# A windowed attention block with MLP: who issues the shift rows and bias rows, and in what order the last stage's data are loaded

## The reference, cut to what matters

```python
B, H, W, C = 8, 16, 16, 192; HEADS = 12; KD = 16; WS = 14; MLP_DIM = 768
h = layer_norm(x, ln1_g, ln1_b)
hp = pad(h, to 28 x 28)                       # 4 windows of 14 x 14 for each image
q, k, v = windows(hp) @ qkv_w + qkv_b         # 12 heads of 16 channels
attn = (q * KD ** -0.5) @ k.T + bias_h[..., :, None] + bias_w[..., None, :]
                                              # bias_h, bias_w: q times relative tables
o = softmax(attn) @ v
x2 = x + unwindow(o @ proj_w + proj_b)
out = x2 + gelu(layer_norm(x2, ln2_g, ln2_b) @ mlp_w1 + mlp_b1) @ mlp_w2 + mlp_b2
```

## Time and profile before

| | us |
|---|---|
| median of 3 runs | 299.33 |
| lowest, highest | 298.60, 302.65 |
| the profiled execution's own time | 298.07 |
| its span in the profile | 296.3 |

### The profile page before, as it was taken

How to read it: one execution, slowest core, us unless ns; L and a number is a source line. 1 busy time by engine, 2 the same in 40 slices (tenths; PEclk the granted TensorE clock), 3 DMA queues, 4 the chain that set the end, 5 groups by cost and what they waited for, 6 DMA issues and landing times.

```text
span 296.3 us, 5322 instructions
## 1 busy us (share of the span) xinstructions
PE 259.4 (88%) x1980; PEld 201.0 (68%) x1980; DVE 164.6 (56%) x435; ACT 128.5 (43%) x233; POOL 92.7 (31%) x143
## 2 busy tenths in 40 slices
PE   0499979899969999999998995899788599999995
PEld 0445458897656777777775673468467478889995
DVE  4875476335686888887887782255499312011011
ACT  1244674433545776676665574352001653141300
POOL 7258480103000333324564412950057700000000
PEclk9999997999977999999998999569557999999999
DMA  6544003374712776777646648601000000101011
GB/s 183 158 120 115 5 2 81 75 173 117 164 39 67 167 175 164 189 183 189 165 134 165 154 82 244 184 19 31 0 0 1 0 2 0 53 2 53 0 55 53
DMA packets 22303, 27.90 MB, mean 94 GB/s; under 512 B 7147, under 2 KB 18515, under 8 KB 22277
## 3 DMA queue, kind: packets, MB, share of 16 engines
q1 hardware_dynamic: 19477, 24.90, 33.3%
q0 software_dynamic: 2272, 2.46, 3.5%
q10 hardware_dynamic: 528, 0.20, 0.3%
HBM read 5.81 MB, written 1.57 MB: 25 GB/s over the span
## 4 chain that ended last, share of the span: by engine, by line
PE 63%; DVE 11%; SPq 10%; DMA 6%; ACT 4%; issue 3%; ACTq 2%; DVEq 0%
PE ps L1289 11%; PE ps L1274 9%; PE ps L977 7%; PE ps L1012 6%; PE ps L1131 5%; PE ps L1067 4%; PE ps L1107 4%; DMA rd<-kst 3%; PE ps L1032 3%; SPq L345 2%; ACT pm L612 2%; DMA qop<-bias 2%; PE ps L1178 2%; DVE var L906 2%; SPq L382 2%
## 5 line engine op out<-in xcount | busy, mean ns | idle before, releaser
L799 DVE TENSOR_REDUCE nmax<-ps 98x2 f32<-98x392 f32 x96 | 52.9, 565 | 24.3 <-PE ps L1067 22.6
L612 ACT ACTIVATE pm<-ps 98x784 f32<-98x784 f32 x48 | 38.9, 825 | 22.7 <-PE ps L1107 22.7
L1067 PE MATMUL ps<-kop,qop 126*98 126x196 f32 x192 | 37.7, 282 | 3.4 <-DMA qop<-bias 1.7
L1067 PEld LDWEIGHTS ps<-kop,qop 126*98 126x98 f32 x192 | 26.3, 171 | 10.3 <-DVE nmax L799 4.1
L1289 PE MATMUL ps<-w2t,gl 128*128 128x192 f32 x192 | 31.7, 326 | 0.0
L1289 PEld LDWEIGHTS ps<-w2t,gl 128*128 128x128 f32 x192 | 31.4, 190 | 0.3
L1107 PE MATMUL ps<-qop,kop 128*98 128x196 f32 x192 | 28.2, 272 | 3.0 <-DMA qop<-shift 2.3
L675 ACT ACTIVATE gl<-ps,b 128x512 f32<-128x512 f32 x24 | 16.4, 688 | 26.5 <-PE ps L1274 26.1
L477 POOL DMA_DIRECT2D den<-osb x11 | 7.1, 643 | 63.1 <-ACT osb L625 63.1
L1107 PEld LDWEIGHTS ps<-qop,kop 128*98 128x98 f32 x192 | 23.1, 180 | 5.0 <-DMA qop<-shift 2.6
L1131 PE MATMUL ps<-pm,v_main 128*17 128x196 f32 x384 | 23.3, 365 | 3.1 <-ACT pm L612 3.0
(11 more groups left out here) (132 smaller groups left out, 458.8 us busy)
## 6 DMA issues: line engine op xcount, KB each, us to landing
qop<-bias SPq DMA_DIRECT2D x8, 343.0 KB
qop<-hl SPq DMA_DIRECT2D x12, 196.0 KB
kop<-hl SPq DMA_DIRECT2D x12, 196.0 KB
bias<-in_x SPq DMA_DIRECT2D x4, 384.0 KB, 4.6
xres<-in_x SPq DMA_DIRECT2D x2, 768.0 KB, 7.9
out<-xn SPq DMA_DIRECT2D x8, 192.0 KB, 2.0
kop<-kst SPq DMA_DIRECT2D x3, 477.8 KB
ot<-osb POOLq DMA_DIRECT2D x44, 32.0 KB, 2.2
```

Source lines behind the costliest of these rows:

```text
L612: a.activation(pm[0:HALF, gi], ps[0:HALF, b0:b0 + 2, 0:2 * WIN], ACT.Exp).then_inc(s["exp_done"], 1)
L799: v_.tensor_reduce(nmax[0:HALF, h % 2, 2 * n:2 * n + 2], ps[0:HALF, bank, 0:2 * WIN].rearrange("p (t k) -> p t k", t=2), AX.X, ALU.max, ne ...
L1067: o = mm(ps[0:HALF, bank, WIN * t:WIN * (t + 1)], q[0:R_MAX, WIN * n + HALF * t:WIN * n + HALF * (t + 1)], kk[0:R_MAX, WIN * n:WIN * (n + ...
```

## The change

Four things are done.
- ScalarE no longer issues the shift rows' transfers; GpSimd does both (`place_main_shifts`, `place_rest_shifts`). Its order in step h is: output of head h − 1, main shift of head h + 1, main low biases of head h + 3, rest shift of head h + 1, rest biases of head h + 3.
- For heads 8 to 11 the high bias rows of the rest half are issued by GpSimd too, which makes four transfers there; SyncE's rest half has four transfers instead of six.
- SyncE loads selector, bias vectors and first projection weight, then the denominators' rows, then w1 and the second projection weight, then the residual in two halves and w2, each of the last three with a semaphore of its own. Who needs the residual waits for it half by half, TensorE waits for w2 at the second layer.
- VectorE takes the last reciprocals at u = 1 instead of u = 5.

```diff
@@ -162,7 +162,7 @@
-            "st_done", "exp_done", "pv_done", "osb_ready", "o_in", "o_in1", "late_in", "rden_ready", "bc_done",
+            "st_done", "exp_done", "pv_done", "osb_ready", "o_in", "o_in1", "late_in", "x_late0_in", "x_late1_in", "w2_in", "rden_ready", "bc_done",
@@ -181,6 +181,7 @@
+        x_late_in = [s["x_late0_in"], s["x_late1_in"]]
@@ -267,15 +268,15 @@
                 (dst[r0:r0 + KD, QUAD * j:QUAD * (j + 1)], osb[32 * j:32 * j + KD, h % 2]) for j in range(4)]
-        def low_biases_loaded(h):
-
-            return 32 * len(range(h, A8 - 1, -RING))
-
-        def operands_loaded(h):
-
-            return 16 * sum(5 if n < A8 else 6 for n in range(h % RING, h + 1, RING))
-
-        N_LATE, N_HIDDEN = 6 * 16, 5 * 16
+        def low_biases_loaded(h, part):
+
+            return 32 * (part + 1) * len(range(h, A8 - 1, -RING))
+
+        def operands_loaded(h, part):
+
+            return 16 * sum(5 if n < A8 else (6, 4)[part] for n in range(h % RING, h + 1, RING))
+
+        N_LATE, N_HIDDEN = 4 * 16, 4 * 16
         block = ctx.enter_context(nc.Block())
@@ -338,7 +339,7 @@
                 if h < A8:
                     sp.dma_start(q[R_BIAS:R_MASK, c0:c1], bias8[bias_row(h):A8 * WS:A8, :, :, c0:c1]).then_inc(sl, 16)
-                else:
+                elif part == 0:
                     n = HEADS - A8
                     for a_ in range(2):
@@ -367,13 +368,12 @@
                     for n in range(HEADS - RING, HEADS):
-                        sp.wait_ge(op_in[n % RING], operands_loaded(n))
-                        sp.wait_ge(rest_in[n % RING], operands_loaded(n))
-                        sp.wait_ge(low_in[n % RING], low_biases_loaded(n))
-                        sp.wait_ge(low_rest_in[n % RING], low_biases_loaded(n))
+                        sp.wait_ge(op_in[n % RING], operands_loaded(n, 0))
+                        sp.wait_ge(rest_in[n % RING], operands_loaded(n, 1))
+                        sp.wait_ge(low_in[n % RING], low_biases_loaded(n, 0))
+                        sp.wait_ge(low_rest_in[n % RING], low_biases_loaded(n, 1))
                     for dst, src in ((sel_in[:], selector), (rb[:, 0], rows[0:1, :].to_broadcast([P, C])),
-                                     (rb[:, 1], rows[1:2, :].to_broadcast([P, C])), (wp0[:], proj_w[0:P]),
-                                     (xres[:, 0:NT // 2], x_tiles[:, 0:NT // 2]), (xres[:, NT // 2:NT], x_tiles[:, NT // 2:NT])):
+                                     (rb[:, 1], rows[1:2, :].to_broadcast([P, C])), (wp0[:], proj_w[0:P])):
                         sp.dma_start(dst, src).then_inc(s["late_in"], 16)
                 if h == HEADS - 2:
@@ -381,9 +381,13 @@
                             sp.dma_start(rd[A8 * l + 4 * k:A8 * l + 4 * (k + 1), 0].bitcast(F32),
                                          den_parts[:, k, l]).then_inc(s["rd0_in"], 16)
-                    for dst, src in ((wp1[0:C - P], proj_w[P:C]), (w10[:], mlp_w1[0:P]), (w11[0:C - P], mlp_w1[P:C]),
-                                     (w11[C - P:P], mlp_w1[P:C]), (w2t[:], mlp_w2.rearrange("(m p) c -> p m c", p=P))):
+                    for dst, src in ((w10[:], mlp_w1[0:P]), (w11[0:C - P], mlp_w1[P:C]), (w11[C - P:P], mlp_w1[P:C]),
+                                     (wp1[0:C - P], proj_w[P:C])):
                         sp.dma_start(dst, src).then_inc(s["hidden_in"], 16)
+                    for c in range(2):
+                        n = slice(NT // 2 * c, NT // 2 * (c + 1))
+                        sp.dma_start(xres[:, n], x_tiles[:, n]).then_inc(x_late_in[c], 16)
+                    sp.dma_start(w2t[:], mlp_w2.rearrange("(m p) c -> p m c", p=P)).then_inc(s["w2_in"], 16)
             sp.wait_ge(s["osb_ready"], HEADS)
             for n, (dst, src) in enumerate(output_rows(HEADS - 1)):
@@ -476,22 +480,40 @@
                     pool.dma_start(dst, src).then_inc(o_in[h % 2], 16)
-            def load_low_biases(h):
+            def load_low_biases(h, part):
                 n = HEADS - A8
+                c0, c1 = ((0, MAIN), (MAIN, T))[part]
                 pool.wait_ge(s["blo_ready"], 16)
-                for part, (c0, c1) in enumerate(((0, MAIN), (MAIN, T))):
-                    pool.wait_ge(s["st_done"], 6 * (h - RING) + (4, 6)[part])
-                    for a_ in range(2):
-                        r0 = 64 * a_ + h - A8
-                        pool.dma_start(qop[h % RING].bitcast(F32)[R_BIAS + 2 * a_ + 1:R_MASK:4, c0:c1],
-                                       bias4[r0:r0 + n * (WS - 1) + 1:n, 1, c0:c1]
+                pool.wait_ge(s["st_done"], 6 * (h - RING) + (4, 6)[part])
+                for a_ in range(2):
+                    r0 = 64 * a_ + h - A8
+                    for l in range(1 - part, 2):
+                        pool.dma_start(qop[h % RING].bitcast(F32)[R_BIAS + 2 * a_ + l:R_MASK:4, c0:c1],
+                                       bias4[r0:r0 + n * (WS - 1) + 1:n, l, c0:c1]
                                        ).then_inc((low_in, low_rest_in)[part][h % RING], 16)
-            for h in range(HEADS - 2):
+            def place_main_shifts(h):
+
+                pool.wait_ge(s["shift_ready"], 2 * h + 1)
+                pool.dma_start(qop[h % RING].bitcast(F32)[R_MAX:ROWS, 0:MAIN], shift[:, h % 2]).then_inc(shift_in[h % 2], 16)
+
+            def place_rest_shifts(h):
+
+                pool.wait_ge(s["shift_ready"], 2 * h + 2)
+                pool.dma_start(qop[h % RING].bitcast(F32)[R_MAX:ROWS, MAIN:T], shift_rest[:, h % 2]).then_inc(rest_shift_in[h % 2], 16)
+
+            place_main_shifts(0)
+            place_rest_shifts(0)
+            for h in range(HEADS - 1):
+                if h:
+                    store_heads_output(h - 1)
+                place_main_shifts(h + 1)
                 if A8 <= h + RING < HEADS:
-                    load_low_biases(h + RING)
-                store_heads_output(h)
+                    load_low_biases(h + RING, 0)
+                place_rest_shifts(h + 1)
+                if A8 <= h + RING < HEADS:
+                    load_low_biases(h + RING, 1)
@@ -500,6 +522,7 @@
             pool.wait_ge(s["rb_ready"], 1)
             for c in range(NCH):
+                pool.wait_ge(x_late_in[c // 2], 16)
                 g.tensor_tensor(xres[:, 4 * c:4 * c + 4], xres[:, 4 * c:4 * c + 4],
                                 rb[:, 0:1].to_broadcast([P, 4, C]), ALU.add).then_inc(s["xpb_ready"], 1)
@@ -586,8 +609,6 @@
                     act.wait_ge(shift_in[h % 2], 16 * (h // 2))
                 a.copy(shift[:, h % 2].bitcast(F32R), ps[0:4 * B, score_bank(main_max_use(h)), 0:HALF]).then_inc(s["shift_ready"], 1)
-                act.wait_ge(s["shift_ready"], 2 * h + 1)
-                act.dma_start(qop[h % RING].bitcast(F32)[R_MAX:ROWS, 0:MAIN], shift[:, h % 2]).then_inc(shift_in[h % 2], 16)
             def rest_shifts(h):
@@ -595,8 +616,6 @@
                     act.wait_ge(rest_shift_in[h % 2], 16 * (h // 2))
                 a.copy(shift_rest[:, h % 2].bitcast(F32R), ps[0:2 * NP, score_bank(rest_max_use(h)), 0:PAIR]).then_inc(s["shift_ready"], 1)
-                act.wait_ge(s["shift_ready"], 2 * h + 2)
-                act.dma_start(qop[h % RING].bitcast(F32)[R_MAX:ROWS, MAIN:T], shift_rest[:, h % 2]).then_inc(rest_shift_in[h % 2], 16)
             def exp_group(h, gi):
@@ -877,7 +896,7 @@
             for u in range(NT // 2):
                 residual_of_eight(u)
-                if u == 5:
+                if u == 1:
                     dve.wait_ge(o_in[0], 5 * 16 * HEADS // 2)
@@ -1050,14 +1069,14 @@
                 q, kk = qop[h % RING], kop[h % RING]
                 if n == 0:
-                    pe.wait_ge(op_in[h % RING], operands_loaded(h))
+                    pe.wait_ge(op_in[h % RING], operands_loaded(h, 0))
                     if h >= A8:
-                        pe.wait_ge(low_in[h % RING], low_biases_loaded(h))
+                        pe.wait_ge(low_in[h % RING], low_biases_loaded(h, 0))
                     pe.wait_ge(const_in[h % RING], 8 * 16)
                 if n == B:
-                    pe.wait_ge(rest_in[h % RING], operands_loaded(h))
+                    pe.wait_ge(rest_in[h % RING], operands_loaded(h, 1))
                     if h >= A8:
-                        pe.wait_ge(low_rest_in[h % RING], low_biases_loaded(h))
+                        pe.wait_ge(low_rest_in[h % RING], low_biases_loaded(h, 1))
                 if h == 0 and n == 4:
                     pe.wait_ge(s["v_ready"], 4)
@@ -1280,6 +1299,7 @@
                 for u in (2 * c, 2 * c + 1):
                     if u == 0:
+                        pe.wait_ge(s["w2_in"], 16)
                         pe.wait_ge(s["x2_ready"], NT // 2)
                     if u >= 2:
                         pe.wait_ge(s["y_ready"], u - 1)
```

## The result

| | us |
|---|---|
| changed kernel, median of 20 runs | 303.6 (300.52 to 307.85) |
| kernel before, median of 20 runs beside them | 299.95 (295.66 to 303.25) |
| ratio, 95% interval | 1.0168 (1.0125 to 1.021) |
| the profiled execution's own time, its span | 302.42, 300.6 |

The account below looks back on a forecast made before the run. TensorE was taken as the bound, busy 7.89 of 8.2 us a head, plus clock dips. From 298.07, −3.0 + 1.0 − 2.5 − 0.6 − 1.1 + 1.6 gave 293.5, forecast as 294.0 us, range 287.0 to 300.5.

Parts of the forecast that it names:

- Part 1: Each head: without ScalarE's two shift issues the exponential starts earlier, 0.31 us a head, −3.0 us over ten heads.
- Part 2: Each head: GpSimd issues the main shift 0.7 us later, landing 2.5 us against 3.1 available; +1.0 us, bounds 0 and +11.
- my own formula: Each head's wait for shift rows: landing L us after issue, a head loses L − 3.1.
- C: Rival: GpSimd's queue paces the heads, shift rows landing after 4.2 us; ten heads lose 11, total 303.5 us; chance 0.1.
- Part 3: Late heads: two bias loads leave SyncE, the bias wait goes and a long head falls to 8.7 us; −2.5 us.
- Part 4: Head 11: wait for shift rows 1.7 instead of 2.3 us (−0.6); wait for denominators' rows goes (−1.1).
- rival B: Head 11: shift rows behind all of the residual, a wait of 4.0 instead of 2.3 us, total 295.8; chance 0.2.
- The tie: Head 11: shift rows and residual are issued within 1.5 us of each other.
- Part 5: Tail after head 11: reciprocals at the second unit block VectorE's residuals, TensorE idles; +1.6 us, up to +3 more if the clock falls.

Follow-up runs that it names:

- e2: Kernel before with only the two shift transfers moved to GpSimd, behind the stores; 302.48 us, ratio 1.0254.
- e5: Changed kernel with only the main shift transfer issued by ScalarE again, the rest shift left on GpSimd; 296.13 us, ratio 0.9898.
- e1: Changed kernel with both shift transfers issued by ScalarE again; 296.75 us, ratio 0.9937.
- e3: Changed kernel with GpSimd issuing the main shift transfer ahead of the five stores; 298.67 us, ratio 0.995.
- e7: Changed kernel with SyncE leaving out low and repeated key and query rows from head 3 on, about half the operand bytes; 299.19 us, measured once.
- e12: Changed kernel with the edits of e3 and e7 together; 297.82 us, measured once.
- e9: e8 with the residual issued ahead of the wait for head 11's shift rows, only the weights behind it; 295.55 us, ratio 0.9845.
- e8: Changed kernel with both shifts on ScalarE, reciprocals at the sixth unit, weights and residual held until head 11's main shift rows land; 295.19 us, ratio 0.9772.
- e4: Changed kernel with the last reciprocals back at the sixth unit (u = 5); 299.82 us, ratio 1.0148.
- e10: e8 with GpSimd storing head 10's output ahead of the four residual additions; 289.67 us, ratio 0.9672.
- e13: e10 with the last reciprocals at the second unit, as in the changed kernel; 293.21 us, ratio 0.9763.

## Why the prediction was wrong, step by step

**Part 1 (ScalarE issues nothing, −3.0) was right.** Seven of eight waits for the exponential went. Where no shift row was late, a head took 7.85 us (the first interval after; twice in e2) against 8.2 with ScalarE issuing (e5); I had said 7.9. The gain is real and did not show in the time, since another wait stood behind it.

**Part 2 (landing 2.5 us, +1.0) is the step that failed.** The issue 0.7 us late and the 3.1 us that remain were right. The landing was 4.1 at the median. I had its bounds, 1.8 and 4.2, and took 2.5, a little above the median of GpSimd's stores (2.2), with the 32 short runs as the only reason. But the shift transfer is issued when SyncE's operand loads are in flight, and from GpSimd it lands late then; the stores themselves still land in 2.1. The page of the changed kernel:

```profile
ot<-osb POOLq DMA_DIRECT2D x44, 32.0 KB, 2.1
```

By my own formula a head loses 4.1 − 3.1 = 1.0 us, and the seven waits of ordinary heads are 1.04 us each. So the formula was right and the term in it was not. By these waits the part cost +7.3; by the intervals about +9, not +1.0 (the nine ordinary heads are 5.8 longer in all, with part 1's 3.0 used up as well). e1, e2 and e5 show that it alone decides: with the main shift on ScalarE all else gives 0.990 to 0.994, and on its own it gives 1.025.

The Trainium skill ("DMA: Bandwidth & Descriptors", section "Issuing engines are not separate DMA queues") holds that another issuer saves sequencer time only. I had weighed C down by it, since C would then depend on load. In this case the issuer matters: the same transfer from ScalarE, beside the same operand loads, landed in 2.6 to 2.7 us instead of 4.1 and made no wait in any head before 11 (e1, e5). The measurement decides. In its other half, that all issuers share the transfer engines, the trace agrees: GpSimd's transfer landed in 2.3 us where SyncE issued nothing. The same page (section "Latency and other measured facts") puts GpSimd's first byte some 0.4 us behind; an estimate by it, 2.2 + 0.4, would have stayed below 3.1 and been wrong too.

What of the 4.1 is what: 2.3 was seen behind five stores with SyncE's queue empty; 3.1 first in the queue under load (e3); 3.8 behind the stores with half the load (e7); 3.6 with both edits (e12). So it takes both, GpSimd's way and traffic beside it, and half of the traffic is enough. The part that stays in e12 is the time from the last data packet to the last semaphore update, 1.7 us against ScalarE's 0.7. Why that is so on GpSimd's way stays open; the transfer's shape was not varied, and the traffic was not taken away whole.

**Part 3 (two bias loads change queue, −2.5) was right to the tenth.** The ninth interval fell from 11.26 to 8.76, there is no wait for bias rows and the clock stayed up. SyncE waits 9.8 us in all for the scores that free its buffers (1.4 before), so it is no longer behind. The slower heads gave it more time, but in e5, with heads of 8.2 us, the ninth interval is 8.72 too. One qualification: with faster heads waits for bias rows came back, 1.3 us in e1, 1.8 in e3 and 1.5 in e9. All but one of them (0.5 us at 171.1 in e3) stand before 135 us, in heads whose bias loads the change leaves with SyncE. In e1 they stand at 117 to 134 us, and the clock stayed at 1.00 there.

**Part 4 (head 11: wait 1.7, then no wait for rows read back) was half right.** The second wait went, as said (−1.1). The wait for shift rows was 3.8 us, a landing of 6.2, which is rival B's size (4.0). The tie came about as forecast, only later: shift rows were issued at 180.43 and the residual at 180.82, and the landing took 6.2 us where I had taken 4.6 (bounds 2.2 and 5.9). The part of the step that failed is its cause, "what counts is whether the residual is issued before the shift rows". e1 has the residual 1.9 us behind and waits 2.9, e9 has the residual ahead and the weights held and waits 3.6, e8 has both held and waits for nothing. So having the residual behind is not enough; the 0.8 MB of weights that I noted as "ahead in any case" are the likely reason, which no run shows by itself.

**Part 5 (reciprocals at the second unit, +1.6) had the right mechanism and too small a size:** +2.6 in this tail (11.31 against 8.72 in e4), and +2.7 to +3.5 in the time between e10 and e13. TensorE idled 2.8 us, near the 3 I expected. The term at fault is the clock: I counted the sixteen products behind the pause at 0.8 us for four (24 matmuls in 4.83 us at full clock) and left the fall of the clock in the upper bound. The clock did fall. The changed kernel's stretches:

```profile
203.50:206.20 2.70, 0.00 (x0) 0.00 (x0) 1.55 (x5) 0.44 (x1) 0.00 (x0) 1.00 0.16 40
206.20:210.80 4.60, 4.57 (x18) 4.25 (x19) 2.02 (x4) 0.00 (x0) 0.00 (x0) 0.63 0.12 25
```

At a mean clock of 0.63 they took 4.53 us instead of 3.2, which is +1.3; the wait for the denominators' rows (1.43 in the earlier trace rows) went, as they came earlier. 2.8 + 1.3 − 1.4 is the +2.7.

The sum with measured terms (of the nine heads' +5.8 only the total is measured, its split between parts 1 and 2 goes by the forecast's −3.0) is −3.0 (part 1) + 8.8 (the nine ordinary heads' 5.8, with part 1's 3.0 given back) − 2.5 + 0.4 (head 11, both waits and its clock) + 2.7 − 0.3 (the spread to the end) = +6.1. The head start of 1.8 us of this profile brings it to +4.3, the difference of the spans. Rival C's sum has +11 for the landing, −1.7 for head 11 and +1.6 for part 5, where these are +8.8, +0.4 and +2.7; its time was met because its errors cancel.

**Chances.** C got 0.1 because its condition was read as one number, the median landing of another transfer, against 3.1. But the bounds were 1.8 to 4.2 and C needs only 3.65. The change put the longest unknown of the case on the chain of every head, ten times. A cost with that multiplier should have had more, by my judgement at least 0.3.

## What to carry to other kernels

A transfer that TensorE waits for in each round belongs on a queue on which its landing has been measured beside the traffic of that round. An empty queue is not enough (e3, e12). Before moving it, take the landing from a transfer of the same kind at the same place in the order, multiply its upper bound by the number of rounds, and give the case beyond the slack a real chance. Here an issue of 0.6 us gave back some 0.3 us a head, and the later landing took 1.0 to 1.2.

Large loads that are not needed soon are best held by a semaphore until the last small transfer on the path has landed; then look at what stands behind the one that waits for them (here a store, which had to move ahead). From e1 to e13, which differ in these two edits alone, the ratio went from 0.9937 to 0.9763, and their intervals do not meet. e10, with the reciprocals at the sixth unit as well, is at 0.9672, where the change as made lost 1.7%.

## What the runs showed of the hardware

- GpSimd's transfer of 12.2 KB in 32 runs landed in 4.1 us at the median behind five stores and 3.1 ahead of them (e3), while the stores of 32 KB around it landed in 2.1. I expected 2.5. The same transfer on ScalarE's queue landed in 2.7 (before) and 2.6 (e1).
- Behind five stores, but with 0.24 of the transfer engines busy, it landed in 2.3 us; with 0.84 busy it took 4.4.
- A small transfer issued 0.5 us behind the start of large loads on another engine's queue was used 6.5 and 7.2 us after its issue (e1: 175.63 to 182.12; e9: 173.21 to 180.40). With no large load ahead it caused no wait (e8).
- With no wait for shift rows TensorE kept 2.4 GHz through head 11, and the whole head took 13.9 us instead of 22. Before, two waits of 2.3 and 1.1 us and the fall of the clock behind them cost the other 8.
- VectorE's cast of 64 columns took 1.72 us in e13 and 0.19 in the changed kernel. It ended at 195.17, as GpSimd's fourth addition on the residual (188.03 to 195.11) did. The Trainium skill ("SBUF — State Buffer", section "SBUF: two separate sides") says that the two engines share a port pair, which one of them holds for a whole instruction; the trace agrees with that for this one cast.
